# Depthwise taps read from PSUM, GpSimd adding two products in 36 units a batch, and a reordered last batch in a one-core transformer and state-space kernel

## The reference, cut to what matters

```python
x = x + attention(layernorm(x))          # 16 heads, latent width 32, causal
x = x + ffn(layernorm(x))                # weights and activations rounded to FP4 by blocks of 16
x = x + ssm(layernorm(x))                # below
x = x + ffn(layernorm(x))

def ssm(x):                              # x has 512 tokens, 512 inner channels, 16 states
    xs, z = split(layernorm(x) @ in_w)
    for each direction (forward, backward):
        xc = silu(conv4(xs) + conv_b)            # 4 taps a channel, causal in its direction
        dt, Bs, Cs = split(xc @ xproj_w)
        dt = softplus(dt @ dt_w + dt_b)
        h[t] = exp(dt[t] * A) * h[t-1] + dt[t] * Bs[t] * xc[t]
        y[t] = sum over 16 states of h[t] * Cs[t]  + xc[t] * D
    return x + (concat(y_fwd, y_back) @ merge_w * silu(z)) @ out_w
```

## Time and profile before

| what | us |
|---|---|
| median of 3 runs | 3976.26 |
| lowest and highest | 3972.01 and 3979.77 |
| the profiled execution | 3971.57 |
| its span, first to last instruction | 3969.8 |
| PE, DVE, ACT, GpSimd busy | 3337.3, 3081.8, 2040.4, 2149.3 |
| ahead of the first scan | 324.2 |
| behind the last unit's start | 111.4 |

### The profile page before, as it was taken

How to read it: one execution, slowest core, us unless ns; L and a number is a source line. 1 busy time by engine, 2 the same in 40 slices (tenths; PEclk the granted TensorE clock), 3 DMA queues, 4 the chain that set the end, 5 groups by cost and what they waited for, 6 DMA issues and landing times.

```text
span 3969.8 us, 40486 instructions
## 1 busy us (share of the span) xinstructions
PE 3337.3 (84%) x12897; PEld 1747.9 (44%) x12897; DVE 3081.8 (78%) x4299; ACT 2040.4 (51%) x3859; POOL 2149.3 (54%) x1330
## 2 busy tenths in 40 slices
PE   7866988798888988899888988889888998888467
PEld 4532543355434554355443454445543454434124
DVE  5345789887897778977887878978789777888884
ACT  2543656346563465645654466534756356554432
POOL 2015655557554665546755475455655366554960
PEclk9988999999999999999999999999999999999588
DMA  3015536645365543735537444554437454473780
GB/s 90 1 43 197 169 128 208 242 140 165 133 215 181 161 160 126 277 120 167 179 124 258 139 162 143 186 205 152 160 127 251 153 162 161 149 254 132 261 260 6
DMA packets 203813, 649.57 MB, mean 164 GB/s; under 512 B 34253, under 2 KB 45520, under 8 KB 197456
## 3 DMA queue, kind: packets, MB, share of 16 engines
q1 hardware_dynamic: 203600, 646.98, 48.5%
HBM read 595.52 MB, written 51.38 MB: 163 GB/s over the span
## 4 chain that ended last, share of the span: by engine, by line
PE 42%; issue 19%; DVE 17%; POOL 13%; ACT 7%; DMA 1%; SPq 1%; POOLq 0%; DVEq 0%; ACTq 0%
PE banks L1342 18%; PE banks L1592 8%; DVE banks L890 6%; PE banks L1371 6%; POOL sb_arena L1026 5%; PE banks L1523 4%; DVE sb_arena L897 3%; PE banks L1347 3%; POOL sb_arena L1037 3%; ACT banks L1309 3%; PE banks L1499 2%; DVE sb_arena L802 1%; ACT sb_arena L1080 1%; POOL sb_arena L938 1%; PE banks L1356 1%
## 5 line engine op out<-in xcount | busy, mean ns | idle before, releaser
L1026 POOL TENSOR_TENSOR sb_arena<-sb_arena 128x1024 f32<-128x1024 f32 x512 | 1211.0, 2366 | 410.7 <-DMA sb_arena<-rows_bc 202.1
L890 DVE TENSOR_TENSOR_SCAN banks<-banks,sb_arena 128x512 f32<-128x512 f32 x1024 | 1198.7, 1216 | 151.1 <-ACT banks L1309 102.9
L1309 ACT ACTIVATE banks<-sb_arena,sb_neg_a 128x512 f32<-128x512 f32 x1024 | 665.5, 682 | 992.3 <-DVE sb_arena L897 981.3
L1592 PE MATMUL banks<-sb_arena,sb_ident 128*128 128x512 f32 x1696 | 892.9, 644 | 326.0 <-DVE sb_arena L897 152.9
L897 DVE TENSOR_TENSOR sb_arena<-banks,sb_arena 128x512 f32<-128x512 f32 x1024 | 652.1, 679 | 0.0
L1080 ACT ACTIVATE sb_arena<-banks 128x512 f32<-128x512 f32 (+4 forms) x752 | 379.3, 518 | 515.6 <-PE banks L1347 363.1
L1592 PEld LDWEIGHTS banks<-sb_arena,sb_ident 128*128 128x128 f32 x1696 | 316.2, 201 | 733.2 <-DVE sb_arena L897 263.4
L1347 PE MATMUL banks<-sb_ident,sb_arena 128*128 128x128 f32 (+1 forms) x2082 | 345.0, 288 | 213.1 <-POOL sb_arena L931 103.6
L1347 PEld LDWEIGHTS banks<-sb_ident,sb_arena 128*128 128x128 f32 (+1 forms) x2082 | 241.8, 145 | 440.3 <-ACT sb_arena L1080 151.0
L753 DVE TENSOR_REDUCE sb_nmax<-banks 128x1 f32<-128x512 f32 (+3 forms) x352 | 224.2, 637 | 238.6 <-PE banks L1526 237.9
L1037 POOL TENSOR_TENSOR sb_arena<-sb_arena 128x512 f32<-128x512 f32 x176 | 223.1, 1268 | 268.1 <-DVE sb_arena L897 250.3
(11 more groups left out here) (128 smaller groups left out, 4066.9 us busy)
## 6 DMA issues: line engine op xcount, KB each, us to landing
sb_arena<-rows_bc SPq DMA_DIRECT2D x1024, 512.0 KB, 4.6
kept_xc<-sb_arena SPq DMA_DIRECT2D x16, 1024.0 KB, 4.8
kept_z<-sb_arena SPq DMA_DIRECT2D x16, 1024.0 KB, 4.9
sb_arena<-kept_z SPq DMA_DIRECT2D x64, 256.0 KB, 4.9
sb_arena<-kept_xc SPq DMA_DIRECT2D x64, 256.0 KB, 5.0
kept_zs<-sb_arena SPq DMA_DIRECT2D x8, 1024.0 KB, 3.8
sb_arena<-kept_zs SPq DMA_DIRECT2D x8, 1024.0 KB, 9.4
sb_xin<-in_x SPq DMA_DIRECT2D x8, 512.0 KB, 7.4
```

The lines of the kernel that those rows point to most:

```text
L890: v.tensor_tensor_scan(products if e == 1 and shared(K) else factors, factors, products, 0.0, ALU.mult, ALU.add).then_inc(V.sem, V.mark("s ...
L1026: nc.gpsimd.tensor_tensor(dBu[K % SLOTS], u[:, p % 2].unsqueeze(1).to_broadcast([P, 2, T]), rows_b[K % BS], ALU.mult).then_inc(G.sem, G.ma ...
L1309: nc.scalar.activation(psum[:, e], dt[:, (K // NQ) % 2], ACT.Exp, scale=neg_a[:, s, m, 2 * q + e:2 * q + e + 1]).then_inc(A.sem, A.mark("d ...
L1592: mm = pe.matmul(psum[:, YB], ident[:, :], dBu[K % SLOTS][:, e], start=(q == 0 and e == 0), stop=(q == NQ - 1 and e == last))
```

## The change

1. **Tables.** `ADDED` goes from units 21 to 42 (22 a batch, in all 8 batches) to units 0 to 4 and 12 to 42 (36 a batch, not in the last batch). `SHARED` goes from none to the odd units from 15 to 63 (25), in the last batch alone. `prep` has 27 visits for 32. `VISITS` is rewritten: `ffn2` takes 6 units for 7, the others the same number in another spread, and `prep` starts one unit earlier and has one more.
2. **prep.** ACT's first tap of each direction reads the PSUM bank directly and takes the last weight; the copy to `xs`, the padding and its memsets go. DVE's taps read PSUM at an offset, over 509, 510 and 511 columns, all three of one block behind each other. The banks are held until both directions' taps have read them, so `z` comes later. The two directions' later steps interleave, on their own `zraw` buffers, with fewer table switches on ACT.
3. **Front.** `soft_in(0)` reads `zraw` in SBUF; `load_z(0)` goes.
4. **Last batch.** The store of batch 6's output and the loads of the merge's gate and residual move from behind the loop to unit 26 of batch 7, and PE does the merge's matmuls in pieces: three blocks in unit 26, one each in units 34, 42, 50 and 58, the last one behind the loop.

```diff
-ADDED, SHARED = range(21, 43), ()
+ADDED, SHARED = tuple(range(5)) + tuple(range(12, 43)), tuple(range(15, NU, 2))
-PREP_EARLY = 25
+PREP_EARLY = 20
+EARLY_MERGE = (26, 34, 42, 50, 58)
 VISITS = {
-    "merge": (1, 1, 0, 3, 2, 0, 2, 3, 3, 3),
+    "merge": (1, 3, 4, 0, 0, 0, 2, 2, 1, 5),
-    "lat": (4, 0, 0, 5, 0, 1, 1, 2, 1, 1, 5, 0, 2, 3, 0, 1),
+    "lat": (3, 1, 0, 3, 1, 2, 1, 2, 0, 3, 1, 1, 1, 2, 2, 3),
...
-        xs = area(DT, TP, start=W)
+        zraw = [area(DT, T, start=W)]
...
         def added(K):
-            return K % NU in ADDED
+            return K < NK - NU and K % NU in ADDED
         def shared(K):
-            return K % NU in SHARED
+            return K >= NK - NU and K % NU in SHARED
...
+            def last_loads():
+                store_out(B - 2)
+                sp.wait_ge(s_out, 16 * (B - 1))
+                sp.dma_start(yg, kept_zs[B - 1]).then_inc(s_yg, 16)
+                sp.dma_start(x[:, :, :], kept_x[B - 1]).then_inc(s_x, 16)
...
+                    for s, first in ((0, 10), (1, 14)):
+                        if first <= i < first + DT:
+                            m = i - first
+                            for k in range(PAD):
+                                if k == 0:
+                                    v.wait_ge(A.sem, A.at("tap", n, 1, m))
                                 else:
                                     v.wait_ge(V.sem, V.at("conv", n, s, m, k - 1))
-                                v.scalar_tensor_tensor(xc[s][:, m], xs[:, m, o:o + T], w_conv[:, s, m, k:k + 1], xc[s][:, m],
-                                                       ALU.mult, ALU.add).then_inc(V.sem, V.mark("conv", n, s, m, k))
+                                late, early = slice(PAD - k, T), slice(0, T - PAD + k)
+                                to, at = (late, early) if s == 0 else (early, late)
+                                v.scalar_tensor_tensor(xc[s][:, m, to], psum[:, prep_bank(m), at], w_conv[:, s, m, k:k + 1],
+                                                       xc[s][:, m, to], ALU.mult, ALU.add
+                                                       ).then_inc(V.sem, V.mark("conv", n, s, m, k))
...
+                z_in = zt if p >= 1 else zraw[0][:, 0]
...
+            def merge_tiles(c, first, end):
+                for k in range(first, end):
+                    pe.wait_ge(V.sem, V.at("ycat", c * NP + k))
+                    if k == 0:
+                        pe.wait_ge(V.sem, V.at("ffn_out", c - 1, 1, TT - 1))
+                    for j in range(DT):
+                        mm = pe.matmul(psum[:, SB[j]], w_merge[:, k, j * P:j * P + P], ycat[:, k],
+                                       start=(k == 0), stop=(k == NP - 1))
+                        if k == NP - 1:
+                            mm.then_inc(E.sem, E.mark("merged", c, j))
...
+                    if 15 <= i < 15 + DT:
+                        m = i - 15
+                        pe.wait_ge(V.sem, V.at("conv", n, 1, m, PAD - 1))
...
+                    if b == B - 1 and k in EARLY_MERGE:
+                        i = EARLY_MERGE.index(k)
+                        merge_tiles(b, i + 2 if i else 0, i + 3)
```

154 lines of the change are left out of this document (72 added, 82 removed).

## The result

The changed kernel takes 3927.23 us (median of 4 runs, 3921.49 to 3928.62), against 3974.14 for the kernel before in the runs beside it: a ratio of 0.9877, 95% interval 0.986 to 0.9894. The prediction had 3812 with a range of 3750 to 3890. The direction was right, the size was not: 50 us of span went, 164 were forecast.

The account below looks back on a forecast made before the run. PE was taken to bound merge and latents, DVE prep, no engine attention. Terms -10 - 56 - 18 - 21 - 28 + 0 - 9 - 22 = -164 from 3971.6, plus 4.7, gave 3812 us, range 3750 to 3890.

Parts of the forecast that it names:

- Prep is DVE's: 53.73 of 56.04: Main part of prep, seven units of a steady batch: DVE, busy 53.73 of 56.04 us, taken as what bounds it.
- -8 a batch: Prep: DVE's 24 taps reading PSUM take 17.9 us instead of 26.6; -8 us in each of 7 batches, -56.
- I count nothing: Prep: PSUM banks held longer delay z and state sums, but DVE is the bound there; counted as no cost.
- Rival C: Prep: taps from PSUM bring nothing, because held banks and ACT's longer pieces take it back; 3868 us, chance 0.05.
- Merge additions: Merge, 6 batches: GpSimd's five additions let PE do one state sum for two; -3 us a batch, -18.
- Latents: -3.5 a batch: Latents, 6 batches: additions in seven of 8 units save PE 6.0 us, taken as -3.5 a batch, -21.
- Attention: -4: Attention, 7 batches: same number of additions, evener spread of visits, fewer PE waits; -4 us each (-12 to +4), -28.
- The last batch: -9: Last batch: units 20 to 49 fall to 3.81 us each without additions; -9 us (ends -11 and +8).
- hidden at full clock: Last batch, unit 26: three merge blocks, 10.3 us of PE, cost nothing at full clock; 9 us late at half clock.
- Front and tail: Front: -10 us, load hop removed and directions interleaved. Tail: -22 us, most of the merge behind the loop gone.
- A: Merge and latents: additions give back what they save, attention stays as it was; 3879 us, chance 0.18.
- D: GpSimd becomes the bound with 98 new additions in batches 0 to 6, kernel slower; 4040 us, chance 0.05.

Follow-up runs that it names:

- e13: Kernel before the change, with DVE's 24 convolution taps done over one column of 512 only: 3969.33 us, ratio 0.9991.
- e6: Changed prep, front and last-batch order only; other stages' tables and additions as before, no shared units, prep's two last steps early: 3928.03 us, ratio 0.9887.
- e14: Changed kernel with DVE's 24 taps done over one column only: 3869.27 us, ratio 0.9735.
- e17: From e8 with prep's visits spread evenly and silus in one piece (3884.81): backward taps of block 0 and z's products earlier; 3905.2 us, ratio 0.9825.
- e9: Changed kernel with ACT's silus of the second direction and of z done for one column of 512 only: 3914.37 us.
- e8: Mended kernel: changed kernel without shared units, prep's last steps at unit 57, silus split, last batch's merge one block at a time: 3886.73 us, ratio 0.9782.
- e5: Changed kernel without the additions of units 12 to 18 in batches 0 to 6: 3963.95 us, ratio 0.9979.
- e7: Changed kernel's additions, merge and latents tables; ffn2 in 7 units, old attention and ffn1 tables, no shared units, prep's last steps early: 3920.53 us, ratio 0.9872.
- e3: Changed kernel without shared units in the last batch, DVE making all second products again: 3913.1 us, ratio 0.9849.
- e1: Changed kernel with prep's last two steps, which hold the late store, moved from units 62 and 63 to unit 57: 3904.61 us, ratio 0.9829.

## Why the prediction was right or wrong

The forecast of 3812 missed by 115 us. Its terms missed by +56 (attention), +46 (prep), +29 (merge), +16 (last batch), +4 (ffn2) and -33 (latents); the ends and ffn1 come to -4.

- **What bounds prep: wrong, and the step that failed.** The step was "Prep is DVE's: 53.73 of 56.04". Without any taps the kernel before takes the same time (e13). PE stood at 15.89 of 15.89 us in the very unit with most taps; the seven-unit row, with PE at 48.05 of 56.04, hid it. So "-8 a batch" for the taps, right to 0.1 us as DVE time (18.0 for 17.9), was worth 0.1 in a batch of 467 (e6). Of the 10 us that prep did bring in the changed kernel 3 are batch 0's and 1.1 each of the other six's; e6, with the old tables, has the 3 as well, but not the 1.1.
- **Held banks: wrong.** "I count nothing" for `z` being late because DVE is the bound. DVE wasn't, and 7 us of taps are on the path in the changed kernel (e14), with PE's products waiting for them; that these waits are how the 7 us get there is argued, and e17 didn't show it. Rival C, with 0.05, named the outcome; of its two reasons ACT's longer pieces are worth at most 1.9 us a batch in prep (e9). The Trainium skill ("VectorE: DVE Perf Modes", "Rules for kernel authors") says for operations on a matmul's output: either accept the plain rate on a PSUM source, or copy first if there will be many. The prediction made of the second half "nought or a loss". Nought was measured, but not by the price of reading PSUM, which is 0.749 us a tap for the 0.742 that one takes from SBUF (median).
- **Merge additions: -3 a batch was near** (43.4 to 40.9 in the mean of e8, 40.3 at best), but SP's queue was not followed. The change moved `kept_z`'s store 15 us later, across the batch's border, in front of SP's wait for it and the next loads, and that took back 0 to 7 us. The prediction's text speaks of no DMA there.
- **Latents: -3.5 a batch, measured -9.0**, of which the additions gave 5.1 and the new table 3.9 (e5). I had cut a computed -6 for waits that the visits behind the products covered, and gave the table nothing. The 33 us that this gave more than forecast hide part of the other misses; that is luck.
- **Attention: -4, measured +3.4, the largest miss.** "The number of additions is the same" was off by one (21 and 22), and "an evener spread" was no way to size it. PE's waits for additions fell by 2.5 us for the 4.7 counted, those for ACT's copies rose by 3.9. The attention starts a unit earlier, and with what GpSimd owes from the stage ahead. Each stage was priced by itself; their border wasn't. With the old table the debt is shown (e7); which of place, table and debt makes the +3.4 of the new one stays open. That no direction could be derived was said; the upper end of +4 was just wide enough for the steady batches, not for batch 0 (+7.6).
- **The last batch: -9 was right for the additions alone** (units 20 to 49 take 118.4 us in e3, and 114.2 without the gap, for 123.3), though their price was not spread over the units, as the mean of 4.11 suggests: most stood at 3.76 before, and two took 7.55. That unit 26's three blocks are "hidden at full clock" was wrong: the granted clock is 1.00 in unit 29 of the changed kernel, and the gap is there all the same, 4.1 us in e3. SP's wait for the store, counted at 3.3 us, was 7.8. And the shared products were counted at nothing where they cost 12 us of the last batch (14 by the medians), although the prediction called GpSimd "tight" at 3.7 of 3.8. Its upper bound of +8 had the sum, at +7.1.
- **Front and tail: right** in place and size. The front's extra 3.5 us were 2.6, which is less than the scatter of the first scan; the tail's -22 was -22.9 in the merge.
- **The rivals.** A (3879) had the right thought for the wrong places: no wait of PE for additions took the saved matmuls' place, a wait of SP and a debt of GpSimd did. D, GpSimd as the bound, is true for some units and never for a stage. None gave 3927: the errors of four terms had one sign, and of the large ones only latents went the other way.

## What to carry to other kernels

- An engine at 96% in a stretch need not be its bound: two queues of the same length look alike. Cut the stretch by single units, see which engines are full in each, and where one can be emptied without changing the order (taps of one column), do that first. It is one run, and it would have taken 56 of the 164 us out of this prediction.
- When steps move, price the border of the stages: what GpSimd owes at the end of one is paid in the next, and the store that moves later on SP stands in front of the next batch's loads. Follow the DMA queue's order as well as the engines'.
- The wait that is seen last moves when its cause is taken away. Compare the sum of the units around it, not the wait.

## What was not expected of the hardware

- Some stages repeat to a hundredth of a us from batch to batch, others, whose order is the same too, don't. Latents took 43.46 us in each of six batches of the changed kernel, attention 145.15 to 145.35 in three of them and 147.17 to 147.45 in the other three.
- Stores of 1024 KB (`kept_z`) land after quite different times. The first direction's took 4.8 to 5.0 us in the steady batches of the kernel before and 9.1 to 9.6 in the changed one, where it is issued 2.4 and 1.9 us (batch 4) behind two other stores of that size; the second direction's took 6.1 to 8.3 and 8.1 to 8.9. What sets it isn't shown: in e1, with the second one moved some 20 us ahead, it takes 9.1 to 10.0.
- The first scan's time scatters between profiles of kernels with the same front: from 314.1 to 317.5 us in those with the silus in one piece, from 316.7 to 320.7 in those with the split. Differences below 4 us should be read from later stretches.
